# Two heads side by side in attention, and the softmax division moved to the out-projection

## The reference

```python
q = einsum('bld,dhk->blhk', ln(x), Wq);  latent = ln(x) @ Wkv_down
k, v = latent @ Wk_up, latent @ Wv_up                    # per head
attn = softmax(causal(q @ k.T / sqrt(64)))
x = x + einsum('bqhd,hdo->bqo', attn @ v, Wout)
x = x + ffn(ln(x))     # 2 rounds: top-2 of 6 experts + 2 shared experts, RMS norm
```

## Time and profile before

| | |
|---|---|
| median of 3 runs | 2847.21 us (2845.93 to 2854.39) |
| the profiled execution | 2857.66 us |
| its span, first to last instruction | 2855.9 us, mean granted clock 0.961 |
| first matmul of scores | 80.45 us |
| last copy of y | 1830.38 us |
| first load of the second stage | 1842.01 us |
| busy | PE 2659.5, DVE 1978.2, ACT 1723.8, POOL 1931.4 us |

### The profile page before, as it was taken

One profiled execution on the slowest core, in us unless ns is written; L12 is line 12 of the kernel. 1 busy time (PEld: TensorE's weight loads), 2 busy tenths in 40 slices (PEclk: granted clock), 3 DMA queues, 4 the chain that ended last, 5 costly groups with the idle time before them and its releaser, 6 DMA issues. The chain is left out here.

```text
span 2855.9 us, 47387 instructions
## 1 busy us (share of the span) xinstructions
PE 2659.5 (93%) x13608; PEld 2215.3 (78%) x13608; DVE 1978.2 (69%) x4391; ACT 1723.8 (60%) x4016; POOL 1931.4 (68%) x1735
## 2 busy tenths in 40 slices
PE   6999999999989999999999999799989998879994
PEld 4788888888768888888888888688878887768883
DVE  7787788788877787887877877265654464753455
ACT  2677777777767777777777777533223442224442
POOL 3698898898878888988988988732442232543234
PEclk8999999999999999999999999899999998889997
DMA  3011111111111101111011010253333451224552
GB/s 72 23 47 39 40 47 39 36 29 43 33 49 29 32 24 25 29 29 27 26 33 25 20 24 20 64 169 126 121 129 117 139 151 57 94 102 141 179 167 85
DMA packets 162161, 191.53 MB, mean 67 GB/s; under 512 B 58093, under 2 KB 126963, under 8 KB 161401
## 3 DMA queue, kind: packets, MB, share of 16 engines
q1 hardware_dynamic: 148600, 154.67, 18.5%
q0 software_dynamic: 12288, 33.57, 3.6%
q10 hardware_dynamic: 1024, 0.26, 0.0%
HBM read 114.45 MB, written 83.14 MB: 69 GB/s over the span
## 5 line engine op out<-in xcount | busy, mean ns | idle before, releaser
L305 POOL TENSOR_TENSOR pl<-pr,ph 128x512 fp32r<-128x512 f32 (+3 forms) x1184 | 1373.5, 1184 | 204.9 <-ACT ph L731 180.5
L728 ACT ACTIVATE pr<-ps 128x512 f32<-128x512 f32 (+3 forms) x1280 | 688.7, 538 | 404.1 <-PE ps L481 162.6
L1003 DVE TENSOR_REDUCE part<-ps 128x1 f32<-128x512 f32 (+3 forms) x1152 | 703.8, 617 | 129.9 <-PE ps L466 115.0
L731 ACT ACTIVATE ph<-ps 128x512 fp32r<-128x512 f32 (+3 forms) x1280 | 688.6, 538 | 0.0
L466 PE MATMUL ps<-k_hi,q_parts 128*128 128x512 f32 (+3 forms) x1280 | 490.5, 384 | 45.8 <-DVE part L1003 36.8
L480 PE MATMUL ps<-q_parts,k_hi 128*128 128x512 f32 (+3 forms) x1280 | 483.0, 377 | 0.2
L481 PE MATMUL ps<-q_row,k_lo 65*128 65x512 f32 (+3 forms) x1280 | 471.7, 369 | 0.0
L466 PEld LDWEIGHTS ps<-k_hi,q_parts 128*128 128x128 f32 x1280 | 243.1, 190 | 136.7 <-DVE part L1003 57.3
L480 PEld LDWEIGHTS ps<-q_parts,k_hi 128*128 128x128 f32 x1280 | 242.3, 189 | 55.0 <-ACT ph L731 7.4
L481 PEld LDWEIGHTS ps<-q_row,k_lo 65*128 65x128 f32 x1280 | 242.9, 190 | 34.1
L1906 POOL DMA_INDIRECT x_slots<-xcur,slot_i x128 | 125.7, 982 | 169.9 <-PE ps L1626 79.8
(11 more groups left out here) (255 smaller groups left out, 4664.7 us busy)
## 6 DMA issues: line engine op xcount, KB each, us to landing
work<-x_slots SPq DMA_DIRECT2D x148, 128.0 KB
e_slots<-work SPq DMA_DIRECT2D x148, 128.0 KB
rec<-recip_rows SPq DMA_DIRECT2D x128, 128.0 KB
y_latent<-y_sums SPq DMA_DIRECT2D x128, 128.0 KB
yg<-y_latent SPq DMA_DIRECT2D x32, 512.0 KB
x_slots<-zero_rows SPq DMA_DIRECT2D x32, 296.0 KB
acc_shared<-accw SPq DMA_DIRECT2D x14, 512.0 KB
accr<-acc_shared SPq DMA_DIRECT2D x12, 512.0 KB, 3.5
```

Source lines behind the costliest of these rows:

```text
L305: eng.tensor_tensor(pl[:, s % RING, 0:w], pr[:, s % PR_RING, 0:w], f32(ph[:, s % RING, 0:w]), ALU.subtract).then_inc(sem, 1)
L728: act.activation(pr[:, s % PR_RING, 0:w], src, ACT.Exp).then_inc(S["probs"], 1)
L731: act.activation(ph[:, s % RING, 0:w], src, ACT.Exp).then_inc(S["probs_hi"], 1)
L1003: ins = dve.tensor_reduce(dst, src[:, 0:w], AX.X, ALU.max)
```

## The change

**Attention.** The two heads of a pair are taken side by side: a block is 256 queries of both heads, 512 columns. There are 8 blocks in a turn, and `SCORE_STEPS` has 72 steps for the pair, 64 of 512 columns and 8 of 256 (the second diagonal step of each block). A diagonal step masks both heads with one instruction. The maxima are cut into near equal pieces (`even_parts`) of up to 512 keys, 80 in a turn as before; they run `LEAD` = 28 pieces ahead, and in eight steps of a turn (8, 17, ..., 71) there are two. DVE makes the low part in every ninth step. The rows of maxima are taken three steps after their last piece. The divide and the load of `rec` are gone; y is stored undivided, and the reciprocals stay in `recip_rows`, which now holds all of them.

**Second stage.** `load_recips` loads the reciprocals of a pair, one DMA for each head, into `recips`, which has one place for even and one for odd pairs. It waits until the pair before in that place is divided (`y_even`, `y_odd`). `divide_y` divides y in place, even pairs on DVE, odd ones on POOL. ACT's split waits for it, and comes after silu 1 instead of ahead of silu 0.

```diff
-SCORE_STEPS = [(qb, kt) for qb in range(QB) for kt in range(TPB * (qb + 1))]
+SCORE_STEPS = [(b, kt) for b in range(NB) for kt in range(2 * b + 2)]
+MAX_STEPS = [(b, head, j, c, at * P, n * P) for b in range(NB) for head in range(2) for j in range(2)
+             for c, (at, n) in enumerate(even_parts(2 * b + j + 1))]
+LEAD = 28
+COPY_AFTER, STORE_AFTER, INVERT_AFTER, RECIP_AFTER = 6, 7, 10, 11
-SPLITS = [(6, 1, 3), (9, 2, 0), (17, 2, 1), (29, 2, 2), (44, 2, 3), (47, 3, 0), (54, 3, 1), (66, 3, 2)]
+SPLITS = [(2, 0, 3, 0), (6, 0, 3, 1), (19, 1, 0, 0), (21, 1, 0, 1), (29, 1, 1, 0), (33, 1, 1, 1), (43, 1, 2, 0), (46, 1, 2, 1)]
-ON_DVE = [s % STEPS in (10, 20, 30) for s in range(2 * STEPS)]
+ON_DVE = [s % 9 == 4 for s in range(STEPS)]
...
+                    out = halves(ps[:, SCORE_BANK + s % 3, 0:width(s)])
+                    pe.matmul(out, khs[p // PAIRS][:, k], qa[:, b, :, off:QW], start=True, stop=False)
+                    pe.matmul(out, kls[p // PAIRS][0:LD + 1, k], qc[:, b, :, off:QW], start=False, stop=True).then_inc(S["scored"], 1)
...
+                    dve.tensor_tensor(src, src, T["mask_kq"][:, None, :].broadcast_to([P, 2, P]), ALU.add).then_inc(S["masked"], 1)
-                def divide(p, half, qb):
-                    dve.wait_ge(S["recip_in"], DMA * (8 * p + 4 * half + qb + 1))
-                    dve.tensor_tensor(y[0:LD, qb, :], y[0:LD, qb, :], rec[:, qb, :], ALU.mult).then_inc(S["normed"], 1)
...
+        recips = F["accr"][:, 1].rearrange("p j d -> p (j d)").rearrange("p (k n) -> p k n", n=BLK)
+        def divide_y(eng, r, pair, sem):
+            i = pair // 2
+            eng.wait_ge(S[f"y_in{i % 2}"], DMA * (2 * r + i // 2 + 1))
+            eng.wait_ge(S[f"recip_in{pair % 2}"], 2 * DMA * (PAIRS // 2 * r + i + 1))
+            rows = y_raw[:, pair % 4, :]
+            eng.tensor_tensor(rows, rows, recips[:, pair % 2, :], ALU.mult).then_inc(sem, 1)
...
+                def load_recips(r, i):
+                    for pair in (2 * i, 2 * i + 1):
+                        done = PAIRS // 2 * r + i
+                        if done:
+                            sp.wait_ge(S["y_odd" if pair % 2 else "y_even"], done)
+                        for head in range(2):
+                            rows = recips[head * LD:(head + 1) * LD, pair % 2, :].rearrange("p (s n) -> p s n", s=2)
+                            sp.dma_start(rows, recip_v[r][pair, :, head, :].unsqueeze(0).broadcast_to([LD, 2, QW])
+                                         ).then_inc(S[f"recip_in{pair % 2}"], DMA)
...
                     if r + 2 < 8:
+                        load_recips(r + 2, 1)
                         load_y(r + 2, 2)
                         load_y(r + 2, 3)
+                        load_recips(r + 2, 2)
...
                         load_x(r + 2)
+                        load_recips(r + 2, 3)
```

More of the change, by code:

```diff
@@ L249, in splits_at, with split_no, row_job @@
         def splits_at(s, last):
-            kept = [j for j in SPLITS if not (last and j[1] >= 2)]
+            kept = [j for j in SPLITS if not (last and j[1] == 1)]
             return [(n, j) for n, j in enumerate(kept) if j[0] == s]
[L253 to L259, removed]
+        def split_no(pair, g, head):
+            return 8 * pair + 2 * g + head
+        def row_job(pair, b):
+            if b >= 3:
+                return jobs_to(pair, "row", 0, b)
+            return jobs_to(pair - 1, "row", 1, b) if pair else first_row_job(b) + 1
         def turns(eng, turn):
@@ new lines, in turn @@
+                def turn(p, first):
+                    for s in range(STEPS):
+                        block_jobs(take_sums, s, STORE_AFTER, p, first)
+                        block_jobs(store, s, STORE_AFTER, p, first)
+                        block_jobs(put_recip, s, RECIP_AFTER, p, first)
+                        n = 4 * p + s // 18
+                        if s % 18 == 4 and n < 16 * B:
+                            clear_slots(n)
+                        if s % 18 == 13 and n < KEPT // 2:
+                            keep(2 * n)
+                            keep(2 * n + 1)
+                        if s % 18 == 13 and 0 <= n - 4 * (PAIRS + 1) < 2 * PAIRS:
+                            bring_back(n - 4 * (PAIRS + 1))
+                        if s == 62 and PAIRS <= p + 2 < TURNS:
+                            stage(p + 2, jobs_to(p, "proj", 1, 3))
+                        if p == PAIRS - 3 and s in (40, 60):
+                            load_next(s // 60)
+                        if p == PAIRS - 2 and s in (26, 40):
+                            load_next(2 + s // 40)
@@ L422, in _ @@
                 for p in range(TURNS):
-                    turn(p, p < TURNS - 2, first=p == 0)
-                store(TURNS - 1, 1, QB - 1)
+                    turn(p, p == 0)
+                for job, after in ((take_sums, STORE_AFTER), (store, STORE_AFTER), (put_recip, RECIP_AFTER)):
+                    late_jobs(job, after)
                 for qb in range(QB):
                     sp.wait_ge(S[f"stored{qb}"], DMA * 2 * TURNS)
+                    sp.wait_ge(S[f"recip_out{qb}"], DMA * 2 * TURNS)
                 sp.wait_ge(S["n_back"], DMA * 2 * PAIRS)
@@ new lines, in _ @@
+                for n in range(16):
+                    max_scores(0, 8 + n)
+                    if n == 1:
+                        first_row(1)
+                    if n == 2:
+                        start_project(2)
+                    if n == 3:
+                        latents(2)
+                    if n == 4:
+                        turn_x(3)
+                    if n == 6:
+                        turn_latents(2)
+                    if n % 2 and n >= 5:
+                        make_m(2 + (n - 5) // 2)
+                    if n == 10:
+                        first_row(2)
+                    if n == 12:
+                        start_project(3)
+                    if n == 13:
+                        latents(3)
```

634 lines of the change are left out of this document (316 added, 318 removed).

## The result

The changed kernel takes 2988.4 us (median of 4 runs, 2985.4 to 2995.5); the kernel before took 2850.8 us beside it. The ratio is 1.0474, 95% interval 1.0453 to 1.0495: slower by 138 us. Forecast were 2935 us and a range of 2835 to 2990. The sign and the main mechanism were right; the size was 53 us short, which lies 1.6 us inside the wide range and outside the forecast's own range of 2880 to 2985.

What follows compares the result with a forecast made beforehand. PE's stream of columns was taken to bound attention, a chain between engines with nearly no slack the second stage. Attention -53, out-projection +120 and stage start +21 gave +88 us: 2945.7 profiled, 2935 us predicted after taking off 10.5; range 2835 to 2990.

Steps and rivals of the forecast that it cites:

- The exposed trip: Out-projection: each engine stands through a whole load of reciprocals, 3.9 us, between two divides using one buffer.
- The block's size: Second stage: each of six projecting blocks takes 20 us more, 120 us in all (bounds 83 and 156).
- The start of the stage: Second stage's first two blocks: 11 us later for the first, +10 for the second, sum 21 (bounds 12 and 30).
- attention's end: After the last scores: the last load, the divide and the wait before the store go, 5.5 us less.
- Attention's columns and waits: Attention's turns: fewer narrow matmuls save 27 us over 16 turns, less waiting for DVE's maxima saves 8 us.
- Turn 6: Attention's turn 6, where DVE also prepares the second sequence: lighter DVE saves 5 us (0 to 15).
- rival three: Attention: steps with two maxima make PE wait on DVE's reads, 8 us a turn; 2995 us in all; chance 0.07.
- The setup: Before turn 0: 28 instead of 40 reads of maxima stand ahead, 7.5 us less.
- that the trips are hidden: Second stage, rival: loads land within other work, only divides count, at most 30 us; 2824 us, faster; chance 0.17.

Runs made afterwards that it cites:

- no_divide: The changed kernel without the division by the softmax sums and its 128 loads of reciprocals: 2800.6 us, 0.9879 of before.
- covered: The changed kernel, still two places for reciprocals, with other work put between the two divides of one engine: 2910.7 us, 1.0275 of before.
- before_no_divide: The kernel before without multiplying y by the reciprocals and without the loads for it: 0.9893 of before.
- four_late: The changed kernel with four reciprocal places, work between divides, DVE's divides 4 and 6 behind gated adds, POOL's held until experts are chosen: 2894.8 us, 1.0088 of before.
- split6: The changed kernel with y divided in attention again, not in the out-projection, and turn 6's layernorm and moments cut in two: 0.9997 of before.
- divide_apart: As split6, with the divides in attention 20 steps behind a block's end instead of 17: 1.0069 of before.

## Why the prediction was right, and where its sizes were off

- **The exposed trip** was right in mechanism, place and length: forecast 3.9 us, measured 3.75, 3.91 and 3.60; layernorm at a+5.6 (a+5.5 forecast), PE's stand before the transposes 4.2 us (4.3). Shown by no_divide, which takes all of the second stage's growth away, and by covered, where PE's wait for layernorm goes. The formula that the prediction quotes from the Trainium skill ("DMA: Bandwidth & Descriptors", Anatomy of one DMA) is given there for DMAs that GpSimd issues; these are SP's, and the sum rightly went by the row of 3.4 us.
- **The block's size** was a little short: 22.3 us a block (20). Three terms: I had pair 4's reciprocals there by a+15; divide 4 began at a+18.6, and from there all came 3.6 us late (gg at a+26.4 instead of a+22.8). Layernorm was taken at its old 1.38 us and took 3.28. And the clock: forecast were 2.8 us and up to 2.3 more, measured 6 a block (42 us over seven).
- **The start of the stage** was mis-sized most: forecast +21 from both blocks, and -5.5 at attention's end. Measured: -7.6 from the last scores to the first load, +15.6 from there to block 0's transposes (11), and +27.1 in the first interval, a full block's price and not 10. I had treated the second block as a repeat of a few trips; it also has y's loads behind the splits, and PE waits 8.8 and 11.8 us in its out-projection, where it waited 2.4 before. Together 167 us from the last scores to block 7's transposes instead of 135.5.
- **Attention's columns and waits** were wrong in the reason, and short in the sum: -16 us from first to last scores instead of -40. The step that failed is "attention is the stream of PE's columns, so work taken from DVE there is worth little". The kernel before without its divides runs its turns in 106.5 us with all the narrow steps still in it; the new form without divides takes 106.4. The 1.5 us a turn are the divides. The forecast had 1.65 a turn from the narrow steps; the waits for maxima are 9.1 us instead of 2.3 in 400 us, 1.8 a turn, so what the wide steps save they seem to give back there (no run separates the two). The forecast also took 4.7 of the 107.7 us for waits; the trace of the kernel before has 4.4 us of waits for maxima in 400 us, 1.2 a turn.
- **Turn 6** had the wrong sign: -5 forecast, +5.0 measured (and +2.4 in turn 7). Layernorm and moments, 2.6 and 2.1 us at a stretch, hold up the maxima; cut in two they cost 13 us less in the new form and 6 in the old. That the new form loses more there goes with its steps of two maxima, rival three's mechanism, but no run takes these away. Outside turns 6 and 7 the turns got shorter, so the rival's total of 2995 us, near the measured one, is near by chance.
- **The setup** gave 13.7 us instead of 7.5.
- **The rivals**: that the trips are hidden was wrong; no_divide shows the price of division and loads together, 157 us in the seven blocks.
- **The 53 us**: attention +24, the stage +32, the setup -6, the tiles behind it -7 make 43; 10 more come from my taking 10.5 us off, since before's profiled execution lay so far above its median. The changed kernel's (2988.9 us) lies at its median. All the same, the errors in the terms are of both signs, and the wide range held by 1.6 us: that it held is partly luck.

## What to carry to other kernels

A load into a buffer that the instruction just before has freed is exposed for its whole trip. Put work that others wait for between the two, or give it a place of its own, and try both: here each gave about 70 us of the seven blocks, and together 98. The first cure leaves the waits as long as they were and moves them to where nobody stands behind them, so a sum of waits doesn't tell what a wait costs. An engine that is busy three quarters of the time can still be the one that is waited for, if another asks it for something every step: its share doesn't tell either, and both the time that is added and the time that it is away at a stretch showed a price. Before work is moved from one stage to another, leave it out of each once: the two runs give its price in both places, here 30 us in attention (before_no_divide against before) and 170 in the second stage (no_divide against the changed kernel).

## What the runs showed of the hardware

DVE and POOL hold each other up for whole instructions when both read two operands from SBUF, and not only then. In the choice of experts DVE adds two tables of 144 columns. In the changed kernel, while POOL divides; then in four_late, with POOL held back:

```profile
2069.28 1.31 POOL L1274 TENSOR_TENSOR yg<-yg,accr 128x512 f32<-128x512 f32 x1
2069.47 1.27 DVE L2140 TENSOR_TENSOR beaten<-beaten,equal 128x144 f32<-128x144 f32 x1
```

```profile
2053.51 0.31 DVE L2148 TENSOR_TENSOR beaten<-beaten,equal 128x144 f32<-128x144 f32 x1
```

1.27 us against 0.31. The same shows in the divides: 64x256 pieces take 0.99 us on average, and a whole 64x512 one took 0.67 where POOL was idle (split6):

```profile
1510.86 0.67 DVE L971 TENSOR_TENSOR y_sums<-y_sums,latents 64x512 f32<-64x512 f32 x1
```

So cutting such an instruction in two doubles the chances to wait: one of 1.35 us became two of 0.99. The Trainium skill ("SBUF — State Buffer", section SBUF: two separate sides) states it as an exclusive lock: whichever of a DVE operation with two SBUF inputs and a GpSimd operation starts first has the shared ports for the whole instruction. These rows agree. I had not weighed that rule, by which each divide in attention can wait out a POOL operation on top of its own time. Layernorm was held up as well, though each of its four instructions reads one tensor from SBUF, with two columns of scalars: 1.38 us in all before and in covered, where POOL is idle then, 3.28 in the block shown above, beside POOL's divide and splits.

And the clock: 117 us more of idle time on PE went with 42 us more of busy time for the same matmuls, at a granted clock of 0.77 instead of 0.95. In this stage a wait cost a third more than its length. In attention it mostly didn't: in divide_apart PE stood 24 of 400 us, in short waits, and the clock was 1.00.
